# Second edge pass of a fused graph-transformer kernel: side steps moved to other visit slots, the row scatter two turns later on GpSimd

## What is computed

```python
def gcn_block(x, edge_index, W, b, n):            # the two convolutions of layer 0
    msg = (x @ W)[src] * norm[:, None]
    return x + relu(segment_sum(msg, dst, n) + b)

def L0_ffn(x, W1, b1, Wg, bg, Wd, bd):            # x is layer-normed, HID = 1024, E = 8
    H = gelu(x @ W1 + b1)
    assign = argmax(softmax(H @ Wg + bg))
    out = 0
    for e in range(E):
        out += where(assign == e, probs[:, e] * (H @ Wd[e] + bd[e]), 0)
```

## Time and profile before

| | |
|---|---|
| median of 3 runs | 4608.51 us (4602.71 to 4615.58) |
| span of the profiled execution, first to last instruction | 4564.2 us |
| outside of the span (median less span) | 44.3 us |
| busy: PE, DVE, ACT, POOL | 74%, 52%, 40%, 59% |
| first pass, first to last gather | 190.5 to 1449.0 us |
| second pass, first to last gather | 1473.3 to 2838.3 us |
| third pass, first to last gather | 3158.0 to 4505.7 us |

### The profile page before, as it was taken

One profiled execution on the slowest core, in us unless ns is written; L12 is line 12 of the kernel. 1 busy time (PEld: TensorE's weight loads), 2 busy tenths in 40 slices (PEclk: granted clock), 3 DMA queues, 4 the chain that ended last, 5 costly groups with the idle time before them and its releaser, 6 DMA issues. The chain is left out here.

```text
span 4564.2 us, 58312 instructions
## 1 busy us (share of the span) xinstructions
PE 3358.6 (74%) x15028; PEld 2583.1 (57%) x15028; DVE 2372.2 (52%) x8487; ACT 1832.8 (40%) x4607; POOL 2695.6 (59%) x2857
## 2 busy tenths in 40 slices
PE   6665556555554576877787778677788888989898
PEld 3444444434443354655665656565577777777776
DVE  5433333333433345555555555354666666666666
ACT  3333334333433333434444434112444445444444
POOL 4366666666665666666666665123566666666663
PEclk8777777777777778888888888787899999999999
DMA  3333333333333333555555555743233333333331
GB/s 110 101 101 101 101 103 102 102 105 101 102 104 98 91 105 120 154 164 168 163 168 167 167 166 162 245 136 94 78 94 94 93 92 95 94 91 94 94 91 52
DMA packets 269355, 532.13 MB, mean 117 GB/s; under 512 B 58645, under 2 KB 166356, under 8 KB 268902
## 3 DMA queue, kind: packets, MB, share of 16 engines
q0 software_dynamic: 139296, 386.65, 28.6%
q1 hardware_dynamic: 129734, 141.79, 9.9%
HBM read 463.88 MB, written 64.34 MB: 116 GB/s over the span
## 5 line engine op out<-in xcount | busy, mean ns | idle before, releaser
L1755 POOL DMA_INDIRECT rows<-table,src_idx x880 | 842.7, 958 | 499.0 <-issue 212.5
L1122 POOL DMA_INDIRECT rows<-table,src_idx x880 | 834.6, 948 | 471.3 <-issue 226.8
L789 POOL DMA_INDIRECT rows<-table,src_idx x880 | 836.5, 951 | 446.5 <-issue 237.5
L915 DVE TENSOR_TENSOR AR<-AR,ps 128x256 f32 x880 | 369.9, 420 | 756.1 <-DMA dst_pad<-rows 427.8
L1285 DVE TENSOR_TENSOR AR<-AR,ps 128x256 f32 x880 | 370.1, 421 | 541.4 <-PE ps L1196 236.2
L2007 PE MATMUL ps<-rows,AR 128*128 128x256 f32 x1760 | 552.4, 401 | 73.4 <-issue 40.1
L2123 DVE TENSOR_TENSOR AR<-AR,ps 128x256 f32 x880 | 369.3, 420 | 271.5 <-PE ps L2007 113.0
L1196 PE MATMUL ps<-rows,work 128*128 128x256 f32 x1168 | 370.9, 432 | 15.3 <-DVE AR L1285 7.6
L2007 PEld LDWEIGHTS ps<-rows,AR 128*128 128x128 f32 x1760 | 289.6, 195 | 161.4 <-issue 95.8
L1237 PE MATMUL ps<-wreg,work 128*128 128x512 f32 x392 | 252.5, 780 | 152.2 <-DVE work L1389 113.8
L844 PE MATMUL ps<-rows,work 128*128 128x256 f32 x880 | 273.7, 451 | 40.9 <-issue 20.4
(11 more groups left out here) (510 smaller groups left out, 6960.3 us busy)
## 6 DMA issues: line engine op xcount, KB each, us to landing
AR<-in_L_ffn_Wd SPq DMA_DIRECT2D x48, 1024.0 KB
rows<-table,src_idx POOLq DMA_INDIRECT x2640
AR<-h_sorted SPq DMA_DIRECT2D x52, 512.0 KB, 3.7
table<-AR SPq DMA_DIRECT2D x147, 128.0 KB
AR<-in_x SPq DMA_DIRECT2D x48, 128.0 KB
out_x<-XN SPq DMA_DIRECT2D x48, 128.0 KB
AR<-in_L_ffn_bd SPq DMA_DIRECT2D x40, 128.0 KB
y_sorted<-AR SPq DMA_DIRECT2D x40, 128.0 KB
```

The source lines that it names most:

```text
L789: g.indirect_dma_start(out=rows[:, u * D:(u + 1) * D], out_offset=None, in_=table[0], in_offset=bass.IndirectOffsetOnAxis(ap=src_idx[:, x: ...
L915: v.tensor_tensor(acc, acc, pair(y), ALU.add).then_inc(s_av, 1)
L1122: g.indirect_dma_start(out=rows[:, u * D:(u + 1) * D], out_offset=None, in_=table[1], in_offset=bass.IndirectOffsetOnAxis(ap=src_idx[:, x: ...
L1755: g.indirect_dma_start(out=rows[:, u * D:(u + 1) * D], out_offset=None, in_=table[2], in_offset=bass.IndirectOffsetOnAxis(ap=src_idx[:, x: ...
```

## The change

In the second pass alone, the side steps get other slots, and some another turn. SP's program is as before, its wait for the scatter of tile i - 5 included. ACT, PE and DVE have one more turn without visits (T + 5 turns), POOL two. No operation is added, dropped or resized. Turn and slot of each step, for tile f and block k:

| step | engine | before | now |
|---|---|---|---|
| layer norm's last step | DVE | f+1, q17 | f+1, q17 |
| transposes of the row | PE | f+2, q0 | f+2, q8 |
| copy | DVE | f+2, q3 | f+2, q9 |
| product with W1 | PE | f+2, q5, 6 | f+3, q3, 4 |
| b1 | DVE | f+2, q9 | f+3, q5 |
| gelu | ACT | f+2, q10 | f+3, q7 |
| transposes | PE | f+2, q12, 13 | f+3, q14, 15 |
| copies | ACT | f+2, q15 | f+3, q16 |
| gate product | PE | f+2, q17, 18 | f+4, q7, 8 |
| route | DVE | f+3, q3, 4 | f+4, q9, 10 |
| rank counts | PE | f+3, q8 | f+4, q17 |
| place | DVE | f+3, q11, 12 | f+5, q0, 1 |
| scatter | POOL | f+4, q16 | f+6, q6 |
| pick of the block | DVE | k+11, q5 to 8 | k+12, q2 to 5 |
| block's transposes | PE | k+13, q1, 2 | k+13, q9, 10 |
| block's copies | ACT | k+13, q4 | k+13, q11 |
| block's product | PE | k+13, q9, 10, 11, 14 | k+14, q0, 1, 5, 6 |
| block's bias | DVE | k+13, q17 | k+14, q8 |

The core of the diff:

```diff
 # POOL
-                    f = i - 4
-                    if q == 16 and has(f):
+                    f = i - 6
+                    if q == 6 and has(f):
                         g.wait_ge(*fps.after(f))
                         g.wait_ge(*fgl.after(f))
...
-                turns(0, T + 4, side, visit)
+                turns(0, T + 6, side, visit)
 # ACT
-                    f, k = i - 2, i - 13
-                    if q == 4 and has_block(k):
+                    f, k = i - 3, i - 13
+                    if q == 11 and has_block(k):
...
-                    if q == 10 and has(f):
+                    if q == 7 and has(f):
                         a.wait_ge(*fhb.after(f))
...
-                    if q == 15 and has(f):
+                    if q == 16 and has(f):
 # PE
-                    f, b = i - 2, i - 13
-                    if q in (1, 2) and has_block(b):
+                    s, f, b = i - 2, i - 3, i - 13
+                    if q in (9, 10) and has_block(b):
...
-                            if has(f - 1):
-                                pe.wait_ge(*fht.after(f - 1))
+                            if has(f):
+                                pe.wait_ge(*fhb.after(f))
+                            else:
+                                pe.wait_ge(*fht.after(T - 1))
...
-                    if q in (9, 10, 11, 14) and has_block(b):
+                    if q in (0, 1, 5, 6) and has_block(b - 1):
...
-                    if q == 0 and has(f):
-                        pe.wait_ge(*srow.after(f))
...
-                    if q in (5, 6) and has(f):
+                    if q in (3, 4) and has(f):
...
-                            if has_block(b):
-                                pe.wait_ge(*xcp.after(b))
...
+                    if q in (7, 8) and has(f - 1):
+                        if q == 7:
+                            pe.wait_ge(*fht.after(f - 1))
...
+                    if q == 8 and has(s):
+                        pe.wait_ge(*srow.after(s))
...
+                    if q in (14, 15) and has(f):
+                        if q == 14:
+                            pe.wait_ge(*fgl.after(f))
+                            if has_block(b):
+                                pe.wait_ge(*xcp.after(b))
...
+                    if q == 17 and has(f - 1):
                         pe.wait_ge(*fsl.after(f - 1))
...
-                    if q in (12, 13) and has(f):
...
-                    if q in (17, QN) and has(f):
 # DVE
-                    s, f, b = i - 1, i - 2, i - 13
-                    if 5 <= q <= 8 and has_block(i - 11):
+                    s, f, b = i - 1, i - 3, i - 14
+                    if 2 <= q <= 5 and has_block(i - 12):
...
-                    if q == 17 and has_block(b):
+                    if q == 8 and has_block(b):
...
-                    if q == 3 and has(f):
-                        v.wait_ge(*ftp.after(f))
+                    if q == 9 and has(i - 2):
+                        v.wait_ge(*ftp.after(i - 2))
...
-                    if q in (3, 4) and has(f - 1):
+                    if q in (9, 10) and has(f - 1):
...
-                    if q in (11, 12) and has(f - 1):
+                    if q in (0, 1) and has(f - 2):
...
-                    if q == 9 and has(f):
+                    if q == 5 and has(f):
                         v.wait_ge(*ffm.after(f))
```

More of the change, by code:

```diff
@@ L1180, in _ @@
                 start(a, xcp)
-                turns(0, T + 4, side, visit)
+                turns(0, T + 5, side, visit)
             @block.tensor
@@ L1240, in side @@
                             ins.then_inc(ffm.sem, 1)
-                    if q == 8 and has(f - 1):
+                    if q in (7, 8) and has(f - 1):
+                        if q == 7:
+                            pe.wait_ge(*fht.after(f - 1))
+                            pe.wait_ge(*fps.room(f - 1))
+                        for k in range(4 * (q - 7), 4 * (q - 6)):
+                            ins = pe.matmul(ps[7][:, 0:NE], hT[:, k * P:(k + 1) * P], wg[:, k, :], start=k == 0, stop=k == HC - 1)
+                        if q == 8:
+                            ins.then_inc(flg.sem, 1)
+                    if q == 8 and has(s):
+                        pe.wait_ge(*srow.after(s))
+                        pe.wait_ge(*fxt.room(s))
+                        pe.transpose(ps[7][:, D:D + P], f_row[:, 0:P], ident[:, :])
+                        pe.transpose(ps[7][:, D + P:2 * D], f_row[:, P:D], ident[:, :]).then_inc(ftp.sem, 1)
+                    if q in (14, 15) and has(f):
[3 more added lines that the diff above has]
+                                pe.wait_ge(*xcp.after(b))
+                        for k in range(4 * (q - 14), 4 * (q - 13)):
+                            ins = pe.transpose(ps[3 + k // 4][:, k % 4 * P:(k % 4 + 1) * P], hr[f % 3][:, k * P:(k + 1) * P], ident[:, :])
+                        if q == 15:
+                            ins.then_inc(ft8.sem, 1)
+                    if q == 17 and has(f - 1):
                         pe.wait_ge(*fsl.after(f - 1))
@@ L1370, in side @@
                 def side(i, q):
[L1371 to L1375 removed]
+                    s, f, b = i - 1, i - 3, i - 14
+                    if 2 <= q <= 5 and has_block(i - 12):
+                        for n in range(2 * (q - 2), 2 * (q - 1)):
+                            pick(i - 12, n)
+                    if q == 8 and has_block(b):
                         v.wait_ge(*xmm.after(b))
@@ L1381, in side @@
                         residual(s, q - 1)
-                    if q == 13 and i == T + 2:
+                    if q == 3 and i == T + 4:
                         v.wait_ge(s_ps, 5 * T)
```

45 lines of the change are left out of this document (13 added, 32 removed).

## The result

| | before | after |
|---|---|---|
| median (7 runs each) | 4607.22 us (4602.71 to 4618.98) | 4591.33 us (4587.02 to 4597.48) |
| ratio to before, 95% interval | | 0.996 (0.9949 to 0.9972) |
| span of the profiled execution | 4564.2 us | 4590.2 us |
| second pass, first to last gather | 1365.0 us, 28.44 a turn | 1357.6 us, 28.28 a turn |
| last gather to the next stage's first transfer | 97.1 us | 107.2 us |

A forecast was written before the change was run, and what follows sets the result against it. The prediction took POOL's second-pass gathers to be held by a late PE, PE and DVE waiting for each other in turn. Terms -153 + 10 = -143 us gave 4465 us from the median 4608.5, range 4404 to 4575.

The forecast's parts named there:

- The bound now: Second pass: POOL's gathers lose 201 us, 4.2 us a turn, to waits for a late PE.
- (1) Wider gaps: Second pass: more slots between dependent steps cut PE's waits, POOL becomes the bound, turn 25.2 us; gain 153 us.
- quarter of the stall: Within the wider gaps' gain: share of POOL's second-pass waiting assumed to stay, 51 us, 1.1 us a turn.
- (2) The scatter: Second pass: place and scatter move 25 to 27 slots later, covered by POOL's lead over PE; cost 0.
- (3) The block's load: Second pass: SP's load, waiting for a later scatter, still reaches PE in time through POOL's lead; cost 0.
- (4) The end: End of second pass: one more turn without visits, last scatter later; +10 us, between 0 and 15.8.
- The 44.3 us outside of the span: Whole kernel: time taken to lie outside the trace's 4564.2 us span, left as it is.
- The rule weighed: Second pass: the skill's rule that GpSimd contends with DVE for SBUF; denser DVE lengthens gathers, 172 us given back at most.
- PE's clock: Rival, second pass: PE granted clock 0.75, turn 26.4 us, 4523 us (4575 with the third pass's turn); chance 0.22.
- The block's loop: Rival, second pass: loop of scatter, block's load, transposes and ring bounds the turn, 30.5 us, 4677 us; chance 0.08.
- Another wait takes the place of the one removed: Rival, second pass: PE's idle time moves to DVE's one-slot steps behind PE, turns stay, 4619 us; chance 0.10.

The follow-up runs named there:

- the decoupled kernel: Changed kernel whose second-pass visits multiply a constant tile (part of W1) and whose gathers wait for no visit, only for the gather 16 before: 5033.66 us, ratio 1.0916.
- its added wait: The decoupled kernel with POOL also waiting for its own last gather before every eighth gather: 4619.81 us, ratio 1.0125.
- its ordinary loads: The decoupled kernel with each indirect gather replaced by an ordinary 128 KB load issued by POOL, without the added wait: 4163.45 us, ratio 0.9024.
- the kernel that is set beside before above: Changed kernel with PE allowed only three pairs of visits ahead of DVE's adds instead of four: ratio 0.9971; its profiled execution took 4559.94 us.

## Why the prediction was wrong, point by point

**The bound now** was misread, and this is the step that failed: "It loses 201 us, 4.2 us a turn, to waits", "So PE is late". The waits are real, their cause was not. I took the names in the releaser column for the cause, and put DVE's 109.1 us behind the DMA name down to PE as well, since a visit needs its rows. What the runs put in its place: POOL's gathers set the turn, and its pauses belong to them. Six edits that took work from PE, DVE or the queues left the turn between 28.0 and 28.3 us; leaving out gathers, or making them ordinary loads, brought 25.1 and 19.2. The turn is 18.33 gathers of 1.25 us, a scatter of 1.3 us, and 113 / 46 = 2.46 pauses (from 1500 to 2800 us, 46 turns) of 2.0 us, 0.3 of it the gap that each gather has anyway: 22.9 + 1.3 + 4.2 = 28.4, against 28.3 measured. That sum only says where the time lies. That the gathers make PE's signals late is shown where they wait for no visit (the decoupled kernel, its added wait, its ordinary loads); that POOL's pauses in the changed kernel are waits for such late signals is carried over by argument, and fits the ordinary loads there. The waits of POOL from 1500 to 2800 us, after:

```profile
POOL rows L1122 <- DMA rows<-dst_pad,newton: 156.3, 72, 3.7
POOL rows L1122 <- PE ps L1196: 66.0, 41, 3.1
```

and before:

```profile
POOL rows L1122 <- PE ps L1196: 151.1, 102, 3.0
POOL rows L1122 <- DMA rows<-dst_pad,newton: 85.2, 46, 3.7
```

148 pauses of 1.6 us became 113 of 2.0 us (112 of 1.9 in the kernel that is set beside before above), 14 to 27 us in all. That is all the change did to POOL.

**(1) Wider gaps, -153 us.** The term came out at 21 us (0.44 us a turn by 48), or 7 by the two profiled executions as they are. Wider gaps do work, but are worth less than was thought even where nothing hides them: PE's wait for the copy is gone, and without the gathers' limit PE needs 19.3 us a turn at the full clock, where I had 19.8. But the gaps give 1.6 us a turn there, not 3.2. "Every step on which PE waits for DVE or ACT has at least 3 slots" did not do it either, since PE's other waits grew. The term was mis-sized by the wrong bound, not by the "quarter of the stall" that I let stay. The third pass, 27.5 us a turn for 22.9 us of POOL's own, and the first with 26.2, could have warned: three passes with quite different work beside the visits have turns that lie within 8% of each other.

**(2) The scatter, cost 0.** No run here tries it alone. Nothing in the waits after speaks against it.

**(3) The block's load, cost 0.** Right as far as it shows: PE's wait for `h_sorted` is not among the waits from 1900 to 2800 us, and a load of an eighth of the weights changed nothing.

**(4) The end, +10 us.** Right: 107.2 - 97.1 = 10.1 us, or 13 with the kernel set beside before above, though by another sum than mine (shorter turns, one more of them, and a wait for the load).

**The 44.3 us outside of the span.** They are not outside of it. In every later run the time is only 1.7 to 2.1 us more than its own span, so the profiled execution before was simply some 42 us shorter than the median. The sum starts from the median and is not moved by that, but the rows that it works from are those of a shorter execution.

**The rule weighed.** Gathers take 947 ns in the median for 946, so what DVE does here does not lengthen them. It is no test of the rule, though: DVE's adds, by far the most of its work beside the gathers, read one input from PSUM (L1285, AR and ps), and only two instructions of 0.4 to 0.5 us a turn read two full-width inputs from SBUF.

**The rivals.** PE's clock did not take it back: it stayed at 0.86, and where nothing held PE it was granted 1.00. The block's loop did not show. "Another wait takes the place of the one removed", 4619 us at a chance of 0.10, came nearest in its turn, which stayed, and had the wrong place: not one of DVE's one-slot steps, but POOL's gathers. As a rival of its own, "the gathers themselves", with the price of the turn that stays, it was missing. That 4591 us lies nearer to this rival's 4619 than to the forecast's 4465 is no merit of the reasoning for it.

## What to carry to other kernels

When an engine idles until another's signal, the row shows when the signal came, not that the other was late: set the recorded end of that other's work beside the release before calling it a bound. Before an order of steps is rebuilt to take away a wait, halve the work of each suspect in turn, the suspect that issues transfers too; here one run with half of the gathers would have shown the bound, and that the gain waits behind it. A wait added to the suspect is as telling as one taken away.

## What the runs showed of the hardware

- The signals of what PE had recorded came late while POOL issued indirect gathers of 128 KB every 1.25 us: in a string of 18 of the decoupled kernel until 1.4 us after the last gather's end, 14 us after the end of PE's last record. In its first string, of 116, they came at one pair of visits in 11.2 us, 40 us after the record, and for 18 us beyond the string's end. With a pause before each eighth gather (300.7 us for 108) most of that lag went. In the changed kernel the pauses are there, and with them 4.2 us of the turn. Ordinary loads of the same size, issued by POOL at 0.53 us each without a gap, held nothing.
- PE's records do not show it: in the piece above they end at 2009.05, and the release is at 2023.38. The Trainium skill (Perfetto Trace Analysis, Tensor Engine Instruction) says that the end of a TensorE record is an estimate and that the signal is pushed only when PSUM has acknowledged the write. The trace agrees in that the release lies behind the record's end; the 14 and 40 us are this case's numbers.
- Open is whether PE's array itself stood still in a string of gathers or only its signals, which part of a gather does it, why the lag outlasts a long string, and why strings in the changed kernel end after some 7 to 8 gathers by themselves (neither the ring of 16 nor the lead of four pairs sets it).
